# Retention layer: the first two abs tiles of a phase added on VectorE, head centring moved into the value weights

## The reference, cut to what matters

```
x  = x + L0(_gn(x))                               # group norm: (g - m) / sqrt(s + 1e-5), 32 groups
q, k, vr = heads(xf @ Wq.T), heads(xf @ Wk.T * SCALING), heads(xf @ Wv.T)     # 8 heads of 32
qk  = einsum('bhqd,bhkd->bhqk', theta_shift(q), theta_shift(k)) * mask
den = clip(abs(qk).sum(-1, keepdims=True), 1.0, 50000.0)
out = einsum('bhqk,bhkd->bhqd', qk / den, vr)
out = (out - out.mean(-1)) / sqrt(out.var(-1) + 1e-5) * ln_g + ln_b            # over the 32 of a head
out = gelu(out) @ Wo.T
```

## Time and profile before

| | before |
|---|---|
| median of 3 runs | 2473.16 us |
| profiled execution, its own time | 2479.87 us |
| its span | 2478.1 us |
| PE busy | 2437.3 us (98%) |
| DVE busy | 1855.7 us (75%) |
| ACT busy | 1464.8 us (59%) |
| POOL busy | 999.8 us (40%) |
| granted TensorE clock | 0.993 of full |

### The profile page before, as it was taken

The page is one execution under the profiler, slowest core; times in us unless marked ns, Lnnn a source line. Parts: engine busy times, 40 slices in busy tenths (PEclk is TensorE's granted clock), DMA queues, the critical chain, the costliest instruction groups (busy, mean ns, idle before and its releaser), DMA issues.

```text
span 2478.1 us, 36390 instructions
## 1 busy us (share of the span) xinstructions
PE 2437.3 (98%) x13326; PEld 1688.8 (68%) x13326; DVE 1855.7 (75%) x2772; ACT 1464.8 (59%) x2063; POOL 999.8 (40%) x695
## 2 busy tenths in 40 slices
PE   8999999999999999999999999999999999999999
PEld 4444444444444444699899878888888888888887
DVE  5888888888888888777777667777666667767775
ACT  3676767676767676666666455555555555555554
POOL 3787777777777777314332301111111100111110
PEclk9999999999999999999999989999999999999999
DMA  7222323232323233244454340000000000000000
GB/s 250 51 78 68 86 69 86 69 86 69 86 69 85 69 86 87 73 66 91 75 93 82 52 111 26 26 26 26 26 26 26 26 26 26 17 17 19 26 26 17
DMA packets 117058, 149.91 MB, mean 60 GB/s; under 512 B 32769, under 2 KB 74121, under 8 KB 116625
## 3 DMA queue, kind: packets, MB, share of 16 engines
q1 hardware_dynamic: 116352, 146.87, 23.5%
q10 hardware_dynamic: 528, 0.72, 0.1%
HBM read 71.93 MB, written 25.26 MB: 39 GB/s over the span
## 4 chain that ended last, share of the span: by engine, by line
PE 89%; DVE 6%; issue 2%; ACT 1%; DMA 1%; POOL 0%; SPq 0%; DVEq 0%; POOLq 0%
PE scores L445 10%; PE scores L1766 9%; PE scores L1768 9%; PE scores L1767 9%; PE pairC L458 8%; PE pairC L475 6%; PE pairD L379 3%; DVE l_prod L586 3%; PE pairC L1766 2%; PE pairC L1767 2%; PE pairC L1768 2%; PE pairD L1766 2%; PE pairD L1768 2%; PE pairD L1767 2%; PE pairD L388 2%
## 5 line engine op out<-in xcount | busy, mean ns | idle before, releaser
L586 DVE TENSOR_TENSOR l_prod<-scores,l_window 128x1024 f32<-128x1024 f32 x512 | 613.6, 1217 | 142.2 <-PE scores L445 134.3
L799 ACT ACTIVATE l_absp<-l_prod 128x1024 f32<-128x1024 f32 x512 | 540.2, 1056 | 293.4 <-DVE l_prod L586 283.6
L445 PE MATMUL scores<-l_qst,l_kst 96*128 96x512 f32 x1024 | 380.9, 462 | 14.0 <-DVE l_prod L586 10.9
L1925 ACT ACTIVATE e_r<-scores,e_bn,e_rs 128x512 f32<-128x512 f32 x256 | 197.9, 779 | 276.7 <-PE scores L1768 276.6
L2156 POOL TENSOR_TENSOR e_xnorm<-e_res,e_scale 128x1024 f32<-128x1024 f32 x16 | 38.5, 2404 | 775.9 <-DMA e_res<-t2T_scratch 775.9
L445 PEld LDWEIGHTS scores<-l_qst,l_kst 96*128 96x128 f32 x1024 | 164.9, 190 | 272.9 <-DVE l_prod L586 132.1
L915 POOL TENSOR_TENSOR l_absp<-l_absp,l_absp 128x1024 f32<-128x1024 f32 x126 | 297.8, 2384 | 14.3 <-ACT l_absp L799 14.0
L2032 DVE CAST e_h1hi<-e_r 128x512 fp32r<-128x512 f32 x256 | 144.0, 563 | 208.2 <-ACT e_r L1925 207.9
L1935 ACT ACTIVATE e_r<-scores,e_bn,e_rs 128x512 f32<-128x512 f32 x250 | 195.1, 781 | 138.8 <-PE scores L1768 137.3
L458 PE MATMUL pairC<-l_prod,l_v 128*32 128x512 f32 x2048 | 268.1, 595 | 0.5 <-ACT l_tA L803 0.5
L2059 DVE TENSOR_TENSOR e_r<-e_r,e_wbc 128x512 f32<-128x512 f32 x250 | 170.9, 690 | 86.2 <-ACT e_r L1935 85.9
(11 more groups left out here) (249 smaller groups left out, 4982.8 us busy)
## 6 DMA issues: line engine op xcount, KB each, us to landing
l_kst<-l_hi SPq DMA_DIRECT2D x248, 64.0 KB, 2.0
l_qst<-l_hi SPq DMA_DIRECT2D x248, 64.0 KB, 2.0
l_xo<-in_x SPq DMA_DIRECT2D x32, 256.0 KB, 3.0
x_scratch<-l_xo SPq DMA_DIRECT2D x32, 256.0 KB, 2.4
l_xa<-x_scratch SPq DMA_DIRECT2D x8, 1024.0 KB, 8.2
l_xr<-x_scratch SPq DMA_DIRECT2D x8, 1024.0 KB, 5.5
t2T_scratch<-l_xt SPq DMA_DIRECT2D x8, 1024.0 KB, 14.9
e_scale<-rows_scratch SPq DMA_DIRECT2D x16, 512.0 KB, 4.1
```

The lines of the kernel that those rows point to most:

```text
L445: mm = nc.tensor.matmul(sc[j][:, s, :], kst[g][0:96, h, 128 * kt:128 * kt + 128], qst[c][0:96, h, :], start=True, stop=True)
L586: nc.vector.tensor_tensor(prod[2 * (S % 2) + j][:], sc[j][:], win[:, 4 * g + 2 * j:4 * g + 2 * j + 2, w0:w0 + QC], ALU.mult).then_inc(prod ...
L799: nc.scalar.activation(absp[S % ABS][j][:], prod[2 * (S % 2) + j][:], ACT.Abs).then_inc(abs_ready, 1)
L1925: nc.scalar.activation(r1[:, m, :], p1[m], ACT.Relu, bias=bn_[0][1][:, m, n:n + 1], scale=rs[0][:, m, n:n + 1]).then_inc(r1_ready, 1)
```

## The change

- The den groups of steps 0 and 1 become one. DVE adds the abs tiles of step 0 to those of step 1 (`add_first_pair`, two additions of 128x1024, both in kt 2, one behind each product). The group (0, 1) is issued in kt 3; kt 2 has no den group any more.
- `head_sums` and `centre` leave DVE in every phase. The columns of wv are centred per head once at the start (`value_sums`, `centre_values`), and the projection of v waits for it. The copy from PSUM to `tA` that `centre` made is a copy on ACT (`take_heads`), behind `squares`, which reads PSUM directly.
- `clip_den` writes its scaled value back to PSUM and clips from there. Those who waited for `den_scaled` (the scaling) to reuse bank `pA` now wait for `den_ready` (the clip, behind it).
- The group norm's `normalise` moves from DVE to ACT (scale and shift in one activation); POOL works out the shift in three more tiny operations per image.

The core of the diff:

```diff
     def den_at(P):
         if P < PHASES - 1:
-            return {2: (0,), 3: (1,), 5: (2, 3), 6: (4,), 7: (5,), 9: (6, 7)}
-        return {2: (0,), 3: (1,), 5: (2, 3), 6: (4,), 7: (5,), 8: (6,), 9: (7,)}
+            return {3: (0, 1), 5: (2, 3), 6: (4,), 7: (5,), 9: (6, 7)}
+        return {3: (0, 1), 5: (2, 3), 6: (4,), 7: (5,), 8: (6,), 9: (7,)}
...
     def a_free(task):
...
-                pe.wait_ge(den_scaled, before[1] + 1)
+                pe.wait_ge(den_ready, before[1] + 1)
...
     def sums(steps):
...
-            if len(steps) == 2:
+            if steps[0] % KT == 0:
+                pe.wait_ge(first_pair_added, 2 * P + 2)
+            elif len(steps) == 2:
                 pe.wait_ge(pair_added, 2 * pair_of[steps[0]] + 2)
...
-        def head_sums(P):
-            dve.wait_ge(b_ready, b_order["nT", P] + 1)
-            nc.vector.tensor_reduce(nsum[:], nT, AX.X, ALU.add).then_inc(nsum_ready, 1)
-        def centre(P):
-            dve.wait_ge(nsum_ready, P + 1)
-            nc.vector.scalar_tensor_tensor(tA[:]..., nsum[:]..., -1.0 / HD, nT, ALU.mult, ALU.add).then_inc(centred, 1)
+        def value_sums():
+            dve.wait_ge(weights_in, 16 * NWEIGHTS)
+            nc.vector.tensor_reduce(nsum[:], wv_heads, AX.X, ALU.add).then_inc(values_centred, 1)
+        def centre_values():
+            dve.wait_ge(values_centred, 1)
+            nc.vector.scalar_tensor_tensor(wv_heads, nsum[:]..., -1.0 / HD, wv_heads, ALU.mult, ALU.add).then_inc(values_centred, 1)
+        def add_first_pair(P, j):
+            dve.wait_ge(abs_ready, 2 * KT * P + 2 + j + 1)
+            nc.vector.tensor_tensor(absp[(KT * P + 1) % ABS][j][:], absp[(KT * P + 1) % ABS][j][:], absp[KT * P % ABS][j][:],
+                                    ALU.add).then_inc(first_pair_added, 1)
...
         def clip_den(P):
             dve.wait_ge(a_ready, a_order["dT", P] + 1)
-            nc.vector.tensor_tensor(dent[:], nT_A[:, :, 0], scales[:, 0, P % 4, :], ALU.mult).then_inc(den_scaled, 1)
+            nc.vector.tensor_tensor(nT_A[:, :, 0], nT_A[:, :, 0], scales[:, 0, P % 4, :], ALU.mult).then_inc(den_scaled, 1)
             dve.wait_ge(den_scaled, P + 1)
-            nc.vector.tensor_scalar(dent[:], dent[:], 1.0, 50000.0, ALU.max, ALU.min).then_inc(den_ready, 1)
+            nc.vector.tensor_scalar(dent[:], nT_A[:, :, 0], 1.0, 50000.0, ALU.max, ALU.min).then_inc(den_ready, 1)
...
+        def take_heads(P):
+            nc.scalar.activation(tA[:].rearrange("p t c -> p (t c)"), pB[:], ACT.Copy).then_inc(heads_taken, 1)
+        def normalise(b, k):
+            act.wait_ge(grstd_ready, 4 * (b + 1))
+            nc.scalar.activation(xn[:, k, :], raw[:, k, :], ACT.Identity, bias=gshift[:, k:k + 1],
+                                 scale=grstd[:, k:k + 1]).then_inc(xn_ready, 1)
```

More of the change, by code:

```diff
@@ L187, in layer0 @@
     stats, mv = sb("stats", [128, 2, 2, 6]), sb("mv", [128, 2, 2])
-    gmean, dmean, gvar, grstd = (sb(n, [128, 2]) for n in ("gmean", "dmean", "gvar", "grstd"))
+    gmean, dmean, gvar, grstd, gshift = (sb(n, [128, 2]) for n in ("gmean", "dmean", "gvar", "grstd", "gshift"))
     mhalf = sb("mhalf", [128, 16])
@@ L373, in b_free @@
             else:
-                pe.wait_ge(centred if before[0] == "nT" else z_ready, before[1] + 1)
+                pe.wait_ge(heads_taken if before[0] == "nT" else z_ready, before[1] + 1)
         def project(w, g, c, parts, to=pA, done=a_ready):
@@ L494, in tensor @@
         project(wk, 0, 1, (0, 1), den, first_made)
+        pe.wait_ge(values_centred, 2)
         project_v(0, 0, (0, 1), num, first_made)
@@ L647, in group_var @@
             nc.vector.tensor_scalar(dmean[:], pA[:, 0:2], GN_EPS, None, ALU.add).then_inc(geps_ready, 1)
[L649 to L654, removed]
         def add_residual(b, c, half):
@@ L695, in vector @@
         group_var(0, 1)
+        value_sums()
         first_normalise()
+        centre_values()
         dve.wait_ge(tables_in, 16 * NTABLES)
@@ L713, in vector @@
             products(S, 0)
-            if kt == 3 and P > 0:
-                centre(P - 1)
+            if kt == 2:
+                add_first_pair(P, 0)
             if kt == 4 and P > 0:
@@ L728, in vector @@
                 aggregate(b + 1)
[L729 to L734, removed]
             if kt == 3 and P > 0:
                 clip_den(P - 1)
+            if kt == 2:
+                add_first_pair(P, 1)
             if kt == 4 and has_kv(P):
@@ L752, in tail @@
         def tail(point):
-            if point == 0:
-                head_sums(last)
-                centre(last)
             if point == 1:
@@ L794, in absolute @@
             if before >= 0:
-                if before in pair_steps:
+                if before % KT == 0:
+                    act.wait_ge(first_pair_added, 2 * (before // KT) + j + 1)
+                elif before in pair_steps:
                     act.wait_ge(pair_added, 2 * pair_of[before] + j + 1)
@@ L810, in squares @@
             act.wait_ge(a_ready, a_order["dT", P] + 1)
-            act.wait_ge(centred, P + 1)
-            nc.scalar.activation(tB[:], tA[:], ACT.Square, scale=HD ** -0.5).then_inc(sq_ready, 1)
+            act.wait_ge(b_ready, b_order["nT", P] + 1)
+            nc.scalar.activation(tB[:].rearrange("p t c -> p (t c)"), pB[:], ACT.Square, scale=HD ** -0.5).then_inc(sq_ready, 1)
+        def take_heads(P):
[4 more added lines that the diff above has]
+                                 scale=grstd[:, k:k + 1]).then_inc(xn_ready, 1)
         def gelu(P):
@@ L858, in scalar @@
             absolute(S, 1)
+            if kt in (1, 2) and P % 4 == 2 and P // 4 + 1 < B:
+                normalise(P // 4 + 1, kt - 1)
             if kt == 0 and P > 0:
@@ L866, in scalar @@
                 squares(P - 1)
+                take_heads(P - 1)
             if kt == 6 and has_kv(P):
@@ L877, in tail @@
                 squares(last)
+                take_heads(last)
             if point == 6:
@@ L929, in scale_heads @@
             pool.wait_ge(fac_step, 4 * P + 4)
+            pool.wait_ge(heads_taken, P + 1)
             tv = tA[:].rearrange("p t (h d) -> p (t h) d", d=32)
```

28 lines of the change are left out of this document (16 added, 12 removed).

## The result

The changed kernel took 2488.22 us, the median of four runs (2487.03 to 2492.37), beside 2472.73 us for the kernel before: a ratio of 1.0064, with a 95% interval of 1.0047 to 1.0082. It is 15.5 us slower. 2485 was forecast, in a range of 2464 to 2515.

The account below looks back on a forecast made before the run. PE was taken to bound the kernel, with DVE just behind. Later k projections 10.8 us plus port waits 1.5 make 12.3 us, so 2473.2 + 12 = 2485 us, range 2464 to 2515.

Parts of the forecast that it names:

- A den group is worth 0.88 us: Step 2 on PE, phase 7: each den group takes 0.88 us; 32 of them are 28.2 us taken from PE.
- The chain on DVE: Step 2's first product to the clip: four products, two additions, scaling, clip; k projection starts 8.01 us after step 1.
- By kind of phase: Later k projection by P % 4: 9.0 us for 0 or 1, 0.3 for 2, 1.5 for 3; together 10.8 us.
- The port: DVE's additions share a port with POOL: 0 to 0.3 us wait per phase, 0.05 taken, 1.5 us in all.
- The rival in which POOL comes first: Step 2: POOL's L893 holds the port, first addition starts 1.4 us late; 38 us more, 2523 us; chance 13%.
- The clip from PSUM: End of DVE's chain before the k projection: clip reading PSUM should take 0.16 us and not wait for the port.
- the term of 52 us: If the new clip did wait for the port, 1.8 us more in PE's path each phase, 52 us in all.
- The other edits: Copy and normalise on ACT, later q cast, centring wv: they fit in ACT's 8.2 us of room, costed at nothing.
- the 0.56 us in 7 phases that normalise gave back: Phases with P % 4 = 2, k projection late by normalise: 7 x 0.56 = 3.9 us, counted in the first rival.
- PE stays the bound: Steps 2 and 3: DVE's chain under 5.8 us, five groups a gain of 28 to 32 us, 2441 to 2445; 10%.

Follow-up runs that it names:

- the run with six groups: The changed kernel with the two additions undone, den groups (0) and (1) back in steps 2 and 3, the other edits kept: 2460.89 us, ratio 0.9941.

## Why the prediction was right, and where its terms were off

- **A den group is worth 0.88 us, and PE bounds the phase.** In the run with the additions in step 6, that step takes 3.91 us in place of 4.77, 0.86 less, where DVE isn't late.
- **The chain on DVE.** Forecast: k projection 8.01 us after step 1, waiting for the clip in every phase. Measured: 8.03 in phase 7, with 29 waits for L619. Undoing the additions puts it at 7.43, halving them at 6.95. Three runs show this step.
- **By kind of phase.** +0.60, +0.04 and +0.21 us were forecast for P % 4 = 0 and 1, 2, and 3. By the starts of the steps they are +0.72 and +0.68, +0.06, and +0.35. Not reckoned was the 0.1 us by which the matmul behind a pause starts slower. 15 x 0.70 + 7 x 0.06 + 7 x 0.35 = 13.4 us, against 10.8.
- **The port.** The forecast that the additions go in between POOL's operations held (L609 at 1.24 and 1.21 in phase 7, L905 and L911 stretched to 2.2), with about 0.0 us of wait in place of 0.05. The rival in which POOL comes first did not occur, but for two additions of 64 at most. It is real all the same: with the additions moved behind the clip they met POOL's and cost over 100 us. DVE's two took 2.17 us more than alone, nearly one addition of POOL's (2.38), and POOL's two took 2.00 more, nearly two of DVE's. The rule of the Trainium skill ("SBUF — State Buffer", "Who interferes with whom"), that the one holds the port for its whole instruction and the other waits, agrees with this.
- **The clip from PSUM.** 0.17 us in all 32 cases, against 0.17 to 2.09 before: the clip does not wait for POOL, and the term of 52 us fell away. Back in SBUF it took 0.93 us at the median. The rule of the Trainium skill ("VectorE: DVE Perf Modes", "Mode 2×_2P"), that the mode with two ports is not to be had for an operand in PSUM, agrees with this. The 0.2 us that waiting for the clip adds to the chain are seen in the steps, and are worth 1.5 us by the medians of the two runs, inside their intervals.
- **The other edits: the term that was mis-sized.** They were costed at nothing but for the 0.56 us in 7 phases that normalise gave back. Without the additions they gain 13 us. The forecast called the clip of 1.94 us hidden, one that PE never waited for. It had made DVE late in step 4 of one kind of phase (0.35 us), and by way of POOL in step 5 of another (0.31 us): there PE waited for the very operation of the earlier trace rows, whose 1.14 us the forecast had read as a sign of the port and not as a cost. Nor is normalise what the 0.56 us come from, or not alone: put back on DVE, it costs nothing once the head sums and the centring are gone. The additions cost more than forecast by about as much: 27 us against the run with six groups, where the forecast's terms give 12.3 + 3.9 = 16. The two errors stand against each other, and it is luck that the sum came out within 3 us. The mechanism, the chain that delays the k projection, is no luck: its start was forecast to 0.02 us.
- **PE stays the bound** (the first rival) needed additions under 0.6 us. With half the width, at 0.6 us of pitch each, the run had 2458 us: only then is it level with six groups or better, and it is still far from the 2441 to 2445 us of that rival.

What stays open: the 6 us that phases 0 to 3 gained from the other edits were read from the steps alone, and no run takes them apart. How the 13 us divide among the head sums, the centring and the clip was not separated by a run either.

## What to carry to other kernels

A busy engine with one small operation that the bounding engine waits for is a chain: before anything is put ahead of that operation, add up what stands between its input and it. Two additions for one den group less came to 33 us less or 102 us more than where they were put first, by what stood behind them: nothing small that PE waits for in most phases, or POOL's additions at the same port and DVE's next product. When an engine's work is offered to another by its idle share, look at each step for what is late there.

## What the runs showed of the hardware that was not expected

- Two additions of 128x1024 in SBUF on DVE and two on POOL at the same time take turns: 4.52 and 6.72 us where alone they take 2.35 and 4.72.
- After some waits of 1 to 2 us on PE, matmuls came back at half the rate (1.91 for 1.02 or 1.03 us) and the granted clock of a 12 us stretch was 0.86. Not every such wait did it: with the additions in step 6, the wait of 1.15 us left the granted clock at 1.00 from 110 to 1009 us. After the changed kernel's wait of 0.70 us it stayed at full too; there only the first matmul was longer, 1.12 for 1.02.
- Waits from a late product can so be dearer than their length: of the 60 us by which the additions alone cost more than expected (109 against 49), about 40 are the clock and 21 the longer wait.
- An operation of DVE on two columns took 1.15 us in place of 0.16 when it met POOL's, and PE waited for it; an edit elsewhere that moved POOL's work away from it took that wait away.
